# Graph layer 1: the edge-to-node member matrices move from VectorE to bf16 products on TensorE, and the order of TensorE's and VectorE's step is edited

## What is computed

```
h = relu(layernorm(x))
q, k, v = h@Wq+bq, h@Wk+bk, h@Wv+bv            # 4 heads of 32
a = softmax over the edges of one receiver of  q[dst]·k[src]/sqrt(32)
x = x + segment_sum(a * v[src], dst) + h@Wskip + bskip
h = relu(layernorm(x))
hs, hr = split(h@W1 + b1)
x = x + hs + segment_sum((hr[src] + ea@We + be) * max(degree,1), dst)
```

## Time and profile before

| | |
|---|---|
| median of three runs | 1656.42 us (1652.73 to 1658.74) |
| the profiled execution | 1654.5 us |
| its span, first to last instruction | 1652.6 us |
| busy, of the span | TensorE 88%, VectorE 81%, GpSimd 65%, ScalarE 61% |
| mean granted TensorE clock | 0.98 of full |

### The profile page before, as it was taken

The page is one execution under the profiler, slowest core; times in us unless marked ns, Lnnn a source line. Parts: engine busy times, 40 slices in busy tenths (PEclk is TensorE's granted clock), DMA queues, the critical chain, the costliest instruction groups (busy, mean ns, idle before and its releaser), DMA issues. The chain is left out here.

```text
span 1652.6 us, 34442 instructions
## 1 busy us (share of the span) xinstructions
PE 1460.2 (88%) x10545; PEld 1260.2 (76%) x10546; DVE 1346.5 (81%) x3688; ACT 1013.4 (61%) x2501; POOL 1081.3 (65%) x1202
## 2 busy tenths in 40 slices
PE   5888888698999999999999984999899989999898
PEld 4667677688888888888898973777677767777676
DVE  8878665299999999999999995777777777777776
ACT  5777888555555656555555522666656656666664
POOL 2554442577777777777777704777777777777774
PEclk9999999899999999999999996999999999999999
DMA  8898898556666666666666616666676666676673
GB/s 219 276 280 299 284 302 263 161 149 178 181 184 187 185 182 182 182 175 187 171 187 178 178 46 162 148 159 161 157 169 160 169 163 153 162 171 160 154 171 95
DMA packets 162552, 302.85 MB, mean 183 GB/s; under 512 B 104113, under 2 KB 107703, under 8 KB 157524
## 3 DMA queue, kind: packets, MB, share of 16 engines
q1 hardware_dynamic: 121503, 201.19, 42.4%
q0 software_dynamic: 40896, 99.90, 24.5%
HBM read 196.84 MB, written 104.12 MB: 182 GB/s over the span
## 5 line engine op out<-in xcount | busy, mean ns | idle before, releaser
L809 POOL DMA_INDIRECT sb_kv<-kv_rows,sb_src_all x500 | 491.1, 982 | 189.9 <-issue 133.4
L837 POOL DMA_INDIRECT sb_kv<-x_rows,sb_src_all x500 | 473.6, 947 | 205.5 <-issue 109.8
L1716 ACT ACTIVATE sb_hn<-sb_xn 100x128 f32<-100x128 f32 x500 | 240.5, 481 | 261.2 <-DMA sb_kv<-x_rows,sb_src_all 201.8
L1719 ACT ACTIVATE sb_vw<-sb_kv 128x128 f32<-128x128 f32 x500 | 239.5, 479 | 0.0
L1644 ACT ACTIVATE sb_hn<-sb_xn,sb_nstat 100x128 f32<-100x128 f32 x500 | 231.9, 496 | 0.0
L1406 DVE COPY sb_hT<-ps_b 128x400 f32<-128x400 f32 x250 | 142.2, 569 | 97.7 <-PE ps_b L2011 97.1
L1803 PE MATMUL ps_b<-sb_w,sb_memberT 128*125 128x256 f32 x800 | 200.7, 389 | 20.7 <-DVE sb_xn L927 11.8
L1666 ACT COPY sb_memberT<-ps_b 100x512 f32<-100x512 f32 x150 | 75.9, 507 | 213.5 <-PE ps_b L1891 213.5
L1803 PEld LDWEIGHTS ps_b<-sb_w,sb_memberT 128*125 128x125 f32 x800 | 145.6, 192 | 44.1 <-issue 16.5
L2011 PE MATMUL ps_b<-sb_member,sb_vw 128*128 128x100 f32 x1000 | 171.9, 276 | 0.0
L2011 PEld LDWEIGHTS ps_b<-sb_member,sb_vw 128*128 128x128 f32 x1000 | 155.7, 196 | 9.8 <-issue 9.8
(11 more groups left out here) (184 smaller groups left out, 3092.0 us busy)
## 6 DMA issues: line engine op xcount, KB each, us to landing
kv_rows<-sb_kv SPq DMA_DIRECT2D x26, 1120.0 KB
sb_xn<-x_rows SPq DMA_DIRECT2D x50, 507.8 KB
sb_xn<-in_x SPq DMA_DIRECT2D x50, 500.0 KB
out_rows<-sb_xo SPq DMA_DIRECT2D x49, 500.0 KB
x_rows<-sb_xo SPq DMA_DIRECT2D x24, 1015.6 KB
sb_kv<-in_edge_attr SPq DMA_DIRECT2D x500, 32.0 KB
sb_kv<-in_x SPq DMA_DIRECT2D x28, 560.0 KB
kv_rows<-sb_xn SPq DMA_DIRECT2D x13, 1120.0 KB
```

The costliest lines, as they stand in the source:

```text
L809: pool.indirect_dma_start(out=kvs[:, k % 4, t, :], out_offset=None, in_=kv_rows, in_offset=bass.IndirectOffsetOnAxis(ap=src_all[:, n:n + 1 ...
L837: pool.indirect_dma_start(out=xs1[:, k % 4, t, :], out_offset=None, in_=x1, in_offset=bass.IndirectOffsetOnAxis(ap=src_all[:, n:n + 1], ax ...
L1716: nc.scalar.activation(hn1[:, t, :], xn1[:, k % 4, t, 0:D], ACT.Relu, scale=xn1[:, k % 4, t, D:D + 1], bias=xn1[:, k % 4, t, D + 1:XW]).th ...
L1719: nc.scalar.activation(hs1[:, t, :], xs1[:, k % 4, t, 0:D], ACT.Relu, scale=xs1[:, k % 4, t, D:D + 1], bias=xs1[:, k % 4, t, D + 1:XW]).th ...
```

## The change

The 128 x 100 member matrix is no longer compared out on VectorE and turned by TensorE. For an edge at node d and a node n, the kernel takes 1 - (d-n)^2 = (1 - n^2) - d^2 + 2dn, shifted to the middle of the tile; it is 1 where d = n and 0 or less elsewhere, so that Relu gives the member matrix. The sum is one bf16 product over 128 rows: `edge_part` holds the edges' factors (d^2 in two bf16 parts, d, and ones), `node_part` the nodes'. Four steps share the 128 rows in cells of 32; each step's `node_part` is zero outside its cell.

- Preparation in the first stage: `node_parts` on GpSimd, `const_row` and `drel_part` on VectorE (11 instructions), four kinds of DMA on the SyncE queue through the new `part_rows` in DRAM.
- VectorE: both `members` go. `scores(k,1)` moves from behind `scores(k,0)` to behind `soft_step` 2.
- TensorE: ten transposes become ten bf16 products (`turned_member`); two new products of 500 columns (`row_member`) make `member` itself. `skip(k-1,0)` moves to the step's start, `turn_weights` moves ahead of `project_q` 2. `turn_h` 0 now waits for the last new evacuation instead of that of `memberT`'s second group.
- ScalarE: the three `copy_member` become Relu of the same size, and two evacuations of 128 x 500 (`member_rows`) are added at the step's end.
- `last_steps` and the third stage are not changed. `brow`, `bpart` and `masked` move into other buffers.

```diff
 # TensorE
+            def turned_member(k, g):
+                first, last = FOURS[g]
+                of_edge, of_node = parts(k)
...
+                    ins = nc.tensor.matmul(banks[(1, 0, 1)[g]][0:NODES, (t - first) * WIN:(t - first + 1) * WIN],
+                                           of_node[:, t, :], of_edge, start=True, stop=True)
...
+            def row_member(k, i):
+                first, last = HALVES[i]
+                of_edge, of_node = parts(k)
+                pe.wait_ge(A.evac, N_ITEM * k + ITEM[("q2", "m1")[i]])
+                nc.tensor.matmul(banks[(2, 0)[i]][:, 0:5 * NODES].rearrange("e (t n) -> e t n", n=NODES),
+                                 of_edge, of_node[:, first:last, :], start=True, stop=True).then_inc(A.item, 1)
...
             def turn_h(k, i):
-                wait(pe, A.evac, N_ITEM * (k - 1) + ITEM[("m1", "m2")[i]])
+                wait(pe, A.evac, N_ITEM * (k - 1) + ITEM[("M1", "m2")[i]])
...
             def step0(k):
+                if prev:
+                    skip(k - 1, 0)
                 if nxt:
                     turn_h(k + 1, 0)
                     turn_h(k + 1, 1)
...
                     project_q(k + 1, 0)
                     project_q(k + 1, 1)
-                    turn_member(k + 1, 0)
+                    turned_member(k + 1, 0)
+                if prev:
+                    turn_weights(k - 1)
+                if nxt:
                     project_q(k + 1, 2)
                 if prev:
-                    turn_weights(k - 1)
-                    skip(k - 1, 0)
                     skip(k - 1, 1)
...
-                    turn_member(k + 1, 1)
-                    turn_member(k + 1, 2)
+                    turned_member(k + 1, 1)
+                    turned_member(k + 1, 2)
+                    row_member(k + 1, 0)
                     gather_q(k + 1, 0)
+                    row_member(k + 1, 1)
                     gather_q(k + 1, 1)
 # ScalarE
-                nc.scalar.copy(memberT[:, k % 2, first:last, :],
+                nc.scalar.activation(memberT[:, k % 2, first:last, :],
...
+            def member_rows(k, i):
+                first, last = HALVES[i]
+                act.wait_ge(A.item, N_ITEM * k + ITEM[f"M{i}"])
+                wait(act, A.agg, 3 * (k - 2))
...
+                nc.scalar.activation(member[:, k % 3, first:last, :],
+                                     banks[(2, 0)[i]][:, 0:5 * NODES].rearrange("e (t n) -> e t n", n=NODES),
+                                     ACT.Relu).then_inc(A.evac, 1)
...
                 relus(k + 2, 9, 10)
+                if nxt:
+                    member_rows(k + 1, 0)
+                    member_rows(k + 1, 1)
 # VectorE
                 if this:
                     scores(k, 0)
                 stats(0)
-                if this:
-                    scores(k, 1)
                 stats(1)
...
                     soft_step(k - 1, 2)
+                if this:
+                    scores(k, 1)
                 stats(4)
-                if nxt:
-                    members(k + 1, 0)
...
                     head_sums(k)
                 stats(13)
-                if nxt:
-                    members(k + 1, 1)
 # SyncE, first stage
+                if b == 23:
+                    const_rows_in()
+                if b == 25:
+                    node_parts_in()
+                if b == 27:
+                    drel_parts_out()
+                if 29 <= b < 29 + QUADS:
+                    edge_parts_in(b - 29)
```

More of the change, by code:

```diff
@@ L52 @@
 HALVES = ((0, 5), (5, 10))
-N_ITEM = 8
-ITEM = {"h0": 1, "h1": 2, "q0": 3, "q1": 4, "m0": 5, "q2": 6, "m1": 7, "m2": 8}
+N_ITEM = 10
+ITEM = {"h0": 1, "h1": 2, "q0": 3, "q1": 4, "m0": 5, "q2": 6, "m1": 7, "m2": 8, "M0": 9, "M1": 10}
+MID = NODES // 2
+QUADS = 4
+CELL = 32
+COLS = (BATCHES + QUADS - 1) // QUADS
 N_SOFT = 8
@@ L162, in build @@
         kvb = sb("kvb", [128, 2 * D])
[L163 removed]
         berow = sb("berow", [1, D])
         bmsg = sb("bmsg", [1, D + 4])
[L166 removed]
         bsplit = sb("bsplit", [128, 5 * D], BF16)
+        edge_part = sb("edge_part", [128, COLS, WIN], BF16)
+        node_part = sb("node_part", [128, QUADS, B, NODES], BF16)
         kv_raw = sb("kv", [128, 4 * B * 2 * D])
@@ L319, in build @@
         chunk_d = sb("chunk_d", [ROWS, 1])
-        masked = sb("masked", [ROWS, HEADS, NODES])
+        masked = spare(ROWS, HEADS * NODES).rearrange("e (h n) -> e h n", h=HEADS)
         run_max = sb("run_max", [NODES, HEADS])
@@ L365, in build @@
         ones_set = sem("ones_set")
+        node_part_made = sem("node_part_made")
+        const_row_step = sem("const_row_step")
+        const_row_in = sem("const_row_in")
+        node_part_in = sem("node_part_in")
+        drel_part_step = sem("drel_part_step")
+        drel_part_out = sem("drel_part_out")
+        edge_part_in = sem("edge_part_in")
         long_done = [sem("L0_long_done"), sem("L1_long_done")]
@@ L587, in segments_out, with const_rows_in, node_parts_in, drel_parts_out @@
                              seg_t.rearrange("r g k e -> r g (k e)")).then_inc(seg_out, 16)
+            def const_rows_in():
+                sp.wait_ge(node_part_made, 6)
+                sp.wait_ge(const_row_step, 5)
+                sp.dma_start(node_part[3 * B:CELL, 0, :, :].rearrange("j t n -> j (t n)"),
+                             const_rows.rearrange("o j t n -> o j (t n)")).then_inc(const_row_in, 16)
+            def node_parts_in():
+                sp.wait_ge(const_row_in, 16)
+                for quad in range(1, QUADS):
+                    sp.dma_start(node_part[CELL * quad:CELL * (quad + 1), quad, :, :], node_part[0:CELL, 0, :, :]
+                                 ).then_inc(node_part_in, 16)
+            def drel_parts_out():
+                sp.wait_ge(drel_part_step, 6)
+                rows = part_rows[0:3 * TILES, :].rearrange("(g r j) e -> r g (j e)", r=ROWS, j=3)
+                for r in PARTS:
+                    sp.dma_start(rows[r, :, :], drel_parts[r, :, :, :].rearrange("r g j e -> r g (j e)")
+                                 ).then_inc(drel_part_out, 16)
+            def edge_parts_in(quad):
+                sp.wait_ge(drel_part_out, 16 * 2)
+                cols = (BATCHES - quad + QUADS - 1) // QUADS
+                rows = part_rows.rearrange("(c q s) e -> q s c e", q=QUADS, s=3 * B)[quad, :, 0:cols, :]
+                sp.dma_start(edge_part[CELL * quad:CELL * quad + 3 * B, 0:cols, :], rows).then_inc(edge_part_in, 16)
             def nodes(k):
@@ L788, in table_stat_math, with node_parts @@
                 pool.tensor_tensor(shift, half, rstd, ALU.mult).then_inc(P.pool_stat, 1)
+            def node_parts(n):
+                cell = node_part[0:CELL, 0, :, :]
+                wait(pool, node_part_made, n)
+                if n == 0:
+                    pool.memset(node_part[:], 0.0).then_inc(node_part_made, 1)
+                elif n == 1:
+                    pool.iota(cell, pattern=[[0, B], [2, NODES]], base=-2 * MID, channel_multiplier=0,
+                              allow_small_or_imprecise_dtypes=True).then_inc(node_part_made, 1)
+                elif n == 2:
+                    pool.affine_select(out=cell, in_=cell, compare_op=ALU.is_equal, fill=0.0, base=-2,
+                                       pattern=[[-3, B], [0, NODES]], channel_multiplier=1).then_inc(node_part_made, 1)
+                elif n < 5:
+                    pool.affine_select(out=cell, in_=cell, compare_op=ALU.not_equal, fill=-1.0, base=-(n - 3),
+                                       pattern=[[-3, B], [0, NODES]], channel_multiplier=1).then_inc(node_part_made, 1)
+                else:
+                    pool.memset(edge_part[:], 1.0).then_inc(node_part_made, 1)
             for m in range(EARLY, PAIRS):
                 table_stat_math(m)
+                if m in (8, 9, 10):
+                    for n in ((0, 1), (2, 3), (4, 5))[m - 8]:
+                        node_parts(n)
                 if m == 5:
@@ L1132, in window_cols, with const_row, drel_part @@
                 ins.then_inc(idx_all, 1)
+            def const_row(n):
+                wait(dve, const_row_step, n)
+                if n == 0:
+                    ins = dve.tensor_scalar(mid_node, iota[0:1, :], -float(MID), None, ALU.add)
+                elif n == 1:
+                    ins = dve.tensor_tensor(mid_square, mid_node, mid_node, ALU.mult)
+                elif n == 2:
+                    ins = dve.tensor_scalar(mid_node, mid_square, -1.0, 1.0, ALU.mult, ALU.add)
+                elif n == 3:
+                    ins = dve.tensor_copy(const_rows[:, 0, :, :], mid_node.unsqueeze(1).to_broadcast([1, B, NODES]))
+                else:
+                    ins = dve.tensor_tensor(const_rows[:, 1, :, :], mid_node.unsqueeze(1).to_broadcast([1, B, NODES]),
+                                            const_rows[:, 0, :, :], ALU.subtract)
+                ins.then_inc(const_row_step, 1)
+            def drel_part(n):
```

(45 more changed lines are left out.)

22 lines of the change are left out of this document (16 added, 6 removed).

## The result

The changed kernel takes 1668.44 us (median of 6 runs, 1666.34 to 1671.99) against 1656.97 for the kernel before, a ratio of 1.0073 with a 95% interval of 1.0058 to 1.0089: 11.5 us slower. The forecast was 1672, slower, range 1658 to 1684. The profiled execution has a span of 1667.2 us.

The account below looks back on a forecast made before the run. A dependency loop through the engines bounds the shorter step, VectorE's work the longer; the change lengthens the loop. 1654.5 + 14.5 (steps) + 2 (preparation) = 1671.0, forecast as 1672 us to allow for the runs' median; range 1658 to 1684.

Parts of the forecast that it names:

- The loop: Attention stage: dependency path across TensorE, ScalarE and VectorE sets the step; shorter step 12.95 to 13.53 us, longer 13.85.
- The new products: TensorE: ten bf16 products at 0.06 us each, bounds 0.055 to 0.11, and two row_member at 0.22 each.
- The waits: Attention steps: VectorE idles about 1.3 us ahead of soft_step 3; TensorE waits 0.7 us or more for the weights.
- "slower still" rival: ScalarE: Relu evacuations dearer than COPY, using up the cover at the step's end; up to 1686 us; chance 0.08.
- T+0.4: ScalarE: last new evacuation ends near 0.4 us after T, the next step's start, covered by skip with 0.7 to spare.
- The faster rival: Attention stage: fullest engine, not the loop, sets the step; GpSimd's 12.65 us decides, 1626 us; chance 0.12.
- The sum over the steps: Attention stage: 22 pairs of steps, 10 x 0.59 + 12 x 0.72 = 14.5 us more.
- the head of the loop: Loop from the step's start to soft_step 3: 0.63+0.95+0.43+0.38 = 2.39 us, plus 1.13 for the moved skip.
- The preparation: First stage: new VectorE and GpSimd work and DMA add between 0 and 6 us, taken as 2.

Follow-up runs that it names:

- taking the relu out: Changed kernel with ScalarE's exponential one place earlier, behind the evacuations of h and ahead of the relu: 1648.17 us, ratio 0.9953 to the kernel before.
- lengthening the loop in the other kernel (the skip): Kernel before with only skip(k-1,0) moved to the start of TensorE's step: 1686.38 us, ratio 1.0198.
- The kernel with the exponential first: Changed kernel with ScalarE's exponential moved ahead of the two evacuations of h and the relu: 1626.28 us, ratio 0.9838 to the kernel before.
- the kernel before with the exponential first: Kernel before with only ScalarE's exponential moved ahead of the evacuations of h: 1717.02 us, ratio 1.0367.

## Why the prediction was right, point by point

- **The loop.** Predicted 13.53 and 13.85 us, measured 13.48 and 13.81. The longer step after, from its rows: 1.09 to `turn_h`, 0.63 to the evacuations, 0.94, 0.39, 0.34 to `soft_step` 3, 3.03 to `weigh`, 2.98 to `finish`, 0.73 to `skip` 2, 1.02 to `turn_alpha`, 2.65 to the next step: 13.80. Such distances add up to the step along any path that leads from one start to the next, so the sum proves nothing by itself. That this path is the loop rests on two things. None of its links has slack in the step shown: each instruction follows the one ahead of it on its own engine at once, or starts when its semaphore comes. And the runs moved it: taking the relu out, lengthening the loop in the other kernel (the skip) and taking the exponential out each changed the step the right way.
- **The new products.** Six turned members take 0.34 us (619.51 to 619.85), 0.056 each: the low end of the bounds, 0.055 to 0.11, was right. The Trainium skill, page "TensorE: Matmul & The Clock Gate", section "Wait — 56ns, not 53.3ns?", gives 55.6 ns at full clock for this shape; the trace agrees. `row_member` takes 0.20 (619.85 to 620.05), taken as 0.22.
- **The waits.** VectorE ahead of `soft_step` 3: about 1.3 was said, 1.82 and 0.77 measured. TensorE for the weights: 0.7 or more was said, 0.99. VectorE's busy share: 44.5 said, 44.79. The Relu evacuations: 1.06 us for two, as COPY's 1.05, so the "slower still" rival had nothing to stand on; they end 0.46 us after TensorE's step start (608.71 against 608.25), T+0.4 was said.
- **The faster rival** was sized for the case that the exponential leaves the loop: 12.65 a step, 1626. The kernel with the exponential first has 12.62 and 1626.28. It wasn't the case here because nothing in ScalarE's order lets it. That the two times agree is partly luck, since the stated bound was GpSimd. GpSimd is close: in that kernel the gathers never wait for `weigh`, and from step 17 to 49 they take 12.57 us a step (521.74 to 923.91). But the kernel's own steps are longer over that stretch (12.65 from one `weigh` to the next), and VectorE waits for a gather only twice past the stage's start, 0.71 and 0.76 us. In the shorter step TensorE has no wait at all, in the longer one 0.4 us of it.
- **The sum over the steps was too large.** 14.5 us were predicted. From one `turn_alpha` to another: the first four steps 61.19 before and 61.41 after, the next sixteen 214.36 and 217.42, the next 28 373.07 and 381.46, the last 11.92 and 11.47. That is 11.2 us. A pair came out at 27.18 to 27.25 on average, not 27.38. In the longer step the head of the loop took 3.39 where 3.52 had been added up, and the link from `soft_step` 3 to `weigh` 3.03 where 2.88 had, 0.11 of that being the longer `soft_step` 5. So two sizes were off with opposite signs. Three of the first pairs, in which that instruction takes 0.22, take only 26.98 to 27.06.
- **The preparation was too small.** 2 us were taken from a bound of 0 to 6; done alone it cost 6.1 (3.3 to 8.5). In the profiled runs the first `turn_alpha` lies at 321.6 to 327.8 us in three kernels without the preparation and at 326.8 to 330.3 in eight with it. The two misses have opposite signs, and that the forecast of 1672 lies 3.6 us from the result is partly luck. How the changed kernel's 11.5 us divide between the two can't be settled better: 11.2 and 6.1 add to 17.3, and the start of the stage differs by several us from run to run. Between the two profiled executions of the result the spans differ by 14.6 us: 2.6 up to the first `turn_alpha` (324.2 to 326.8), 11.2 in the steps, and 0.9 behind the last one. In the kernel with the preparation alone the first `turn_alpha` comes 6.1 later than before (330.3), and the steps then take 657.7 and not 660.5, so that part of a late start is made up. Which of the eleven instructions and four kinds of DMA costs the time wasn't tried.

## What to carry to other kernels

Where several engines run hand-ordered programs, look for a path that leads from one step's start to the next and tiles it, before believing the fullest engine: its length, and not an engine's load, can be the period, and work taken off beside it brings nothing. Look for slack in its links, since a sum of start-to-start distances always comes out. Follow what a moved instruction is put ahead of on its own engine, and what that engine's consumer has queued behind it: here a cover for a 0.5 us wait sat 1.1 us ahead of an exponential two engines away. And test a suspected loop by moving one instruction that costs no engine anything.

## What the runs showed of the hardware that was not expected

TensorE's clock fell in the middle of a stage in which it was granted in full for most of the time. In the kernel before with the exponential first, after a step with an idle 1.63 us, the granted clock of a 4 us stretch was 0.63 and products ran at the time of the lower level, 1.2 GHz, for part of it; the longer step grew from 14.70 to 16.37 us. The same idle time at 512 us, in the same kernel, brought no such fall. In the changed kernel, with idle times of 0.99, the clock stayed at 1.00 through the attention stage's steady steps.
